# Context transposed once and kept in DRAM, and the first group of the last stage opened in two halves of rows

## What is computed

```python
x = x + L0_xattn(layernorm(x), ctx)        # one head, per sequence
x = x + L0_ffn(layernorm(x))               # 8 experts of 512, best 2 per row, and a shared one
x = x + L1_xattn(layernorm(x), ctx, mask)  # 16 heads of 64: keys and values from ctx
x = x + L1_ffn(layernorm(x))               # relu, 128 -> 512 -> 128
```

## Time and profile before

| | us |
|---|---|
| median of 3 runs | 1432.9 (1428.61 to 1436.73) |
| the profiled execution: its time | 1434.55 |
| the profiled execution: its span | 1432.9 |
| PE busy in it | 1315.9 (92%) |
| DVE, ACT, POOL busy in it | 983.2, 779.6, 523.0 |

### The profile page before, as it was taken

How to read it: one execution, slowest core, us unless ns; L and a number is a source line. 1 busy time by engine, 2 the same in 40 slices (tenths; PEclk the granted TensorE clock), 3 DMA queues, 4 the chain that set the end, 5 groups by cost and what they waited for, 6 DMA issues and landing times.

```text
span 1432.9 us, 41859 instructions
## 1 busy us (share of the span) xinstructions
PE 1315.9 (92%) x16184; PEld 1149.3 (80%) x16185; DVE 983.2 (69%) x2418; ACT 779.6 (54%) x1480; POOL 523.0 (36%) x560
## 2 busy tenths in 40 slices
PE   4999999985999999757899999999999999999977
PEld 3888888874999999745787888788878888888866
DVE  3788888765655555425787778777877777778673
ACT  3455555532555555335565656656665666566642
POOL 2366666653122222273424342434243424331000
PEclk9899999997999999969999999999999999999998
DMA  3111112604222222120110111011101110110000
GB/s 85 40 59 60 60 60 64 183 30 120 78 77 77 76 78 73 59 70 25 28 28 15 29 35 28 14 31 33 30 13 31 32 31 14 31 28 13 2 9 16
DMA packets 90348, 66.85 MB, mean 47 GB/s; under 512 B 24816, under 2 KB 81136, under 8 KB 90192
## 3 DMA queue, kind: packets, MB, share of 16 engines
q1 hardware_dynamic: 78592, 38.51, 9.5%
q0 software_dynamic: 11600, 26.10, 6.1%
HBM read 40.73 MB, written 23.86 MB: 45 GB/s over the span
## 4 chain that ended last, share of the span: by engine, by line
PE 48%; DVE 3%; issue 2%; POOL 2%; ACT 1%; DMA 0%; another core or an unknown queue 0%; DVEq 0%; ACTq 0%; POOLq 0%
PE c_ps_w L83 21%; PE c_ps_w L1414 8%; PE c_ps_s L1380 5%; PE c_ps_w L1403 5%; PE c_ps_w L1431 4%; PE c_ps_w L1389 3%; PE c_ps_w L1333 2%; POOL c_back L1262 1%; DVE c_shifted L1711 1%; DVE c_shifted L1708 1%; DVE c_r_max L1710 1%; POOL k_X L1272 0%; DMA c_back<-sorted_y,k_y_row_of 0%; ACT c_o_t L1563 0%
## 5 line engine op out<-in xcount | busy, mean ns | idle before, releaser
L1283 POOL TENSOR_TENSOR c_rstd<-c_var,c_minus_half 128x1 f32<-128x1 f32 x64 | 35.8, 560 | 484.0 <-DVE c_var L1691 484.0
L91 POOL DMA_INDIRECT sorted_x<-f_XN,f_slot_of x128 | 130.7, 1021 | 81.4 <-PE a_ps_w L749 30.7
L1414 PEld LDWEIGHTS c_ps_w<-c_wo,c_o_t 128*128 128x128 f32 x1024 | 124.7, 196 | 24.1 <-ACT c_o_t L1563 20.9
L1414 PE MATMUL c_ps_w<-c_wo,c_o_t 128*128 128x128 f32 x1024 | 129.5, 281 | 14.4 <-ACT c_o_t L1563 10.9
L1262 POOL DMA_INDIRECT c_back<-sorted_y,k_y_row_of x128 | 125.9, 983 | 39.0 <-issue 34.8
L1535 ACT ACTIVATE c_q_t<-c_ps_w 128x512 f32<-128x512 f32 x128 | 74.5, 602 | 117.7 <-PE c_ps_w L83 116.3
L1055 PE MATMUL d_ps_y<-e_w_all,d_h_t 128*128 x1136 | 138.1, 275 | 0.3 <-ACT d_h_t L1009 0.3
L1055 PEld LDWEIGHTS d_ps_y<-e_w_all,d_h_t 128*128 128x128 f32 x1136 | 132.8, 192 | 0.5 <-issue 0.5
L1708 DVE TENSOR_TENSOR c_shifted<-c_ps_s,c_mask 128x1024 f32<-128x1024 f32 x64 | 78.4, 1224 | 76.6 <-PE c_ps_s L1380 70.9
L940 POOL DMA_DIRECT2D sorted_y<-d_y_rows x71 | 51.9, 731 | 210.8 <-DVE d_y_rows L971 206.5
L1009 ACT ACTIVATE d_h_t<-d_ps_h,d_biases 128x256 f32<-128x256 f32 x284 | 111.4, 475 | 4.4 <-PE d_ps_h L83 4.2
(11 more groups left out here) (238 smaller groups left out, 3545.8 us busy)
## 6 DMA issues: line engine op xcount, KB each, us to landing
d_x_rows<-sorted_x SPq DMA_DIRECT2D x71, 128.0 KB, 2.1
sorted_y<-d_y_rows POOLq DMA_DIRECT2D x71, 128.0 KB, 2.2
k_X<-in_x SPq DMA_DIRECT2D x16, 256.0 KB
a_q_rows<-in_ctx SPq DMA_DIRECT2D x16, 256.0 KB
c_ctx_rows<-in_ctx SPq DMA_DIRECT2D x16, 256.0 KB
out<-k_X SPq DMA_DIRECT2D x16, 256.0 KB, 2.3
sorted_x<-f_XN,f_slot_of POOLq DMA_INDIRECT x128
e_w_all<-in_L_ffn_w SPq DMA_DIRECT2D x1, 2048.0 KB
```

Of the source, the lines that this page charges most:

```text
L91: pool.indirect_dma_start(out=sorted_x, out_offset=bass.IndirectOffsetOnAxis(ap=slot_of[:, choice, t:t + 1], axis=0), in_=XN2[:, t, :], in ...
L1414: last = pe.matmul(w[:, 0:D], o_t[:, j, :], wo[:, j, :], start=(j == 0), stop=(j == J - 1))
```

## The change

1. **Context kept.** Stage a stores each `q_t` (the transposed context) to DRAM as `ctx_cols[g]` with a transfer of SP; ACT's next write of `q_t` waits for it (`ctx_stored`). Stage c loads `ctx_cols[g]` into `ctx_raw` and splits from there: its 16 sets of four context transposes and their PSUM banks are gone. `XN2` becomes a ring of four groups (`xn2`), whose reuse waits for the scatters.
2. **Experts' weights earlier.** SP issues them after the loads that follow groups 5, 8, 11 and 12 of stage a.
3. **Stage d.** Eleven tiles are written out. The four `low` parts are made one after each of tiles 3 to 6; the context of group 0 is loaded and split there (ACT after tile 7, DVE after tile 8). DVE copies the first three tiles' weights ahead of its first `low_x`. ACT runs one `Gelu` on a single column before its first copy.
4. **Opening of stage c.** Group 0's rows are added by DVE tile by tile (`add_first`), and normalised, transposed and projected in two halves of two tiles (`xna`, `xnb`; `qa`, `qb`), with scores(0) between them. Keys, values and queries of group 1 are placed among tiles 0 to 3. Group 1 is gathered into the unused `h_t`.

The core of the diff:

```diff
+            for g in range(G):
+                sp.wait_ge(ct_ready, 3 * g + 3)
+                sp.dma_start(ctx_cols[g], q_t[:]).then_inc(ctx_stored, 16)
...
+                if g >= 1:
+                    act.wait_ge(ctx_stored, 16 * g)
                 act.wait_ge(full, full_at("qt", g))
                 act.copy(q_t[:], bank("qt", g)[:]).then_inc(ct_ready, 1)
...
+def high_context(act, ctx_t, raw):
+    c = batches_of(raw)
+    act.copy(ctx_t.high[:, :, 0:NB, :], c)
+    return act.copy(ctx_t.high[:, :, NB, :], c[:, :, 0, :])
...
+                if 3 <= n < 3 + len(layer1):
+                    low_layer1(n - 3)
+                if n == 8:
+                    dve.wait_ge(ctx_high, 1)
+                    low_context(dve, ctx_t, ctx_raw).then_inc(ctx_low, 1)
...
+            def add_first(k):
+                dve.wait_ge(gathered_0[k], 16 * 2)
+                for choice, w in enumerate((w_first, w_second)):
+                    step(dve.scalar_tensor_tensor(row_of(k), back[:, choice, k, :], w[:, k:k + 1], row_of(k), ALU.mult, ALU.add))
...
-            ctx_transposes(0)
             project_k(0, range(J))
-            for p in range(GT):
+            for p in range(GT - 1):
                 project_v(p, range(2))
+            first_transposes("xna", 0)
+            project_v(GT - 1, range(2))
+            project_first("qa", 0)
+            scores(0)
+            project_k(1, (0, 1))
+            first_transposes("xnb", 1)
+            project_k(1, (2, 3))
+            project_first("qb", 1)
+            scores(1)
+            project_k(1, (4, 5))
+            transpose_probs(0)
+            project_k(1, (6, 7))
+            values(0)
+            project_v(GT, range(2))
             pe.wait_ge(w_loaded, 16 * 4)
-            xn_transposes(0)
-            project_q(0, range(J))
+            out_projection(0)
+            scores(2)
+            transpose_probs(1)
+            project_v(GT + 1, range(2))
+            values(1)
             xn_transposes(1)
-            ctx_transposes(1)
+            project_v(GT + 2, range(2))
+            out_projection(1)
+            project_q(1, (0, 1, 2, 3))
+            scores(3)
...
-                if k == 3 and g + 2 < G:
-                    ctx_transposes(g + 2)
```

More of the change, by code:

```diff
@@ L100, in phase_a @@
     MAX_TILES = NT * P // SLOTS
[L101 removed]
+    BANKS, AHEAD, KEPT = 8, 3, 4
     with ExitStack() as ctx:
@@ new lines, in filled @@
+            yield ("xna", 0)
+            yield from (("v", GT - 1, h) for h in range(2))
+            yield from (("qa", 0, n) for n in range(J // 2))
+            yield from (("k", 1, j) for j in (0, 1))
+            yield ("xnb", 0)
+            yield from (("k", 1, j) for j in (2, 3))
+            yield from (("qb", 0, n) for n in range(J // 2))
+            yield from (("k", 1, j) for j in (4, 5))
+            yield from (("pt", 0, half) for half in range(2))
+            yield from (("k", 1, j) for j in (6, 7))
@@ L1136, in filled @@
+            yield from (("q", 1, j) for j in (4, 5))
+            yield from (("pv", 2, b) for b in range(NB))
+            yield from (("q", 1, j) for j in (6, 7))
+            yield ("o", 2)
+            yield from (("v", GT + 3, h) for h in range(2))
+            yield ("xn", 2)
+            for p in range(GT, NT):
                 yield from filled_in_slot(p)
@@ L1153, in filled_in_slot @@
                 yield from (("k", g + 1, j) for j in (5, 6))
-            if k == 3 and ended:
+            if k == 3:
                 yield ("down", g - 1, 0)
-            if p > 0:
-                yield from (("pt", p - 1, half) for half in range(2))
+            yield from (("pt", p - 1, half) for half in range(2))
             if k == 0 and coming:
@@ L1334, in transposes, with first_transposes @@
                 last.then_inc(full, 1)
-            def ctx_transposes(g):
-                pe.wait_ge(loaded, 16 * (g + 1))
-                transposes(begin("ctx", g), ctx_rows)
+            def first_transposes(name, half):
+                ks = range(half * GT // 2, (half + 1) * GT // 2)
+                pe.wait_ge(x_normed, ks[-1] + 1)
+                w = begin(name, 0)
+                for n, k in enumerate(ks):
+                    last = pe.transpose(w[:, n * P:(n + 1) * P], xn_rows[:, k, :], ident[:])
+                last.then_inc(full, 1)
             def xn_transposes(g):
@@ L1346, in x4_transposes, with project_first @@
                 transposes(begin("x4", g), xn4_rows)
+            def project_first(name, half):
+                emptied(("xna", "xnb")[half], 0)
+                HW = GW // 2
+                for n in range(J // 2):
+                    w = begin(name, 0, n)
+                    for a in range(2):
+                        j = 2 * n + a
+                        last = split_matmul(pe, w[:, a * HW:(a + 1) * HW], wq, xn_t, lambda c: c[:, j * P:(j + 1) * P],
+                                            lambda x: x[:, half * HW:(half + 1) * HW])
+                    last.then_inc(full, 1)
             def project_q(g, js):
@@ L1528, in high_x4, with take_first @@
                 act.copy(xn_t.high[:], bank("x4", g)[:]).then_inc(high_ready, 1)
+            def take_first(name, half):
+                HW = GW // 2
+                for n in range(J // 2):
+                    act.wait_ge(full, full_at(name, 0, n))
+                    act.mul(q_t[0][:, 2 * n:2 * n + 2, half * HW:(half + 1) * HW],
+                            bank(name, 0, n)[:].rearrange("p (a c) -> p a c", a=2), Q_SCALE).then_inc(free_of(name, 0, n), 1)
             def take_q(g, js):
```

457 lines of the change are left out of this document (294 added, 163 removed).

## The result

The changed kernel takes 1423.5 us (median of 4 runs, 1422.5 to 1426.1) against 1433.0 for the kernel before (4 runs). The ratio is 0.9935, with a 95% interval of 0.9917 to 0.9954: 9.4 us or 0.65% faster. Forecast were 1403 (1391 to 1420). The profiled execution took 1424.52 us, its span is 1422.7.

A forecast was written before the change was run, and what follows sets the result against it. The prediction took PE as the bound inside the stages, with PE's waits at the stage borders as the rest. Terms -22.4 - 5.0 - 2.3 = -29.7 us from the median 1432.9 gave 1403 us, range 1391 to 1420.

The forecast's parts named there:

- Opening, -22.4: Opening of stage c: new order laid out on traced times brings scores(4) earlier; -22.4 us, bounds 14 to 31.3.
- The rival of DVE's chain: Opening of stage c: DVE's serial chain becomes the new bound, gaining only 5 to 14 us; 1411 to 1421, chance 0.17.
- Middle, -5.0: Middle of stage c: PE is the bound, so removing four context transposes in 13 groups gives -5.0 us, bounds 0 and 5.7.
- The rival "the idle time only changes place": Stage c: the opening's waits return in groups 1 and 2, whose gathers POOL does later; 1428 to 1436, chance 0.05.
- Stage d, -2.3: Stage d, 376 to 380: low parts spread one per tile hide beside the loop, removing 2.35 us of PE idle; -2.3 us.
- Stage a, 0: Stage a: ACT's wait for the store of `q_t` and the earlier weight loads cost nothing; 0, from -1 to +3 us.
- Sum: Whole kernel: opening, middle and stage d together, -22.4 - 5.0 - 2.3 = -29.7 us.
- the scores of tile 4 came in time: Sign in stage c's opening: scores(4) expected near 673; the prediction is wrong if they come after 685.
- DVE's time did not grow: Sign in stage c: the prediction is wrong if DVE's time in a group grows.
- A group's period near 47.6: Sign in the middle of stage c: a group's period expected near 47.6 us, where it was 48.1.
- the border at 603 to 604: Sign at stage c's border: expected 2.3 us earlier, if stage a and the start of stage d stand.

The follow-up runs named there:

- e7: e4 with the gathers in group 1's slots and the two ahead of its sums also set between the short matmul runs; 1379.7 us, ratio 0.9608.
- e5: Kernel before, with only POOL's gathers in a group's second and third slot waiting until PE has done the slot's values; 1406.6 us, ratio 0.9787.
- e4: Changed kernel, with POOL's gathers in the second and third slot of groups 2 to 12 waiting for the slot's values; 1391.8 us, ratio 0.9687.
- e10: e5, with ACT copying the previous tile's values ahead of its exp in a group's first slot; 1398.5 us, ratio 0.9701.
- e9: e7, with ACT copying the previous tile's values ahead of its exp in a group's first slot; 1366.4 us, ratio 0.9492.
- e12: Changed kernel as it is, run once more; 1428.2 us, ratio 0.9915 to the kernel before.
- e8: Changed kernel, with the gathers of groups 3 to 15 replaced by plain POOL transfers of 128 rows (wrong rows); 1383.3 us, ratio 0.9640.

## Why the prediction was wrong

The direction was right, the size was not: 9.4 us instead of 29.7. By its own steps:

- **Opening, -22.4.** Right in order and size. Measured -21.3, from the end of stage d to tile 4. The order of events was as written: keys to scores(0) 18.4 us (laid out 18.3), the 4.2 us of waiting for group 1's rows (laid out 4). Keys to scores(4) took 71.5 us instead of 67.4; those 4 us are scores(1), held up by gathers, and without most of that (e7) tiles 0 to 4 take 4.1 us less. The rival of DVE's chain did not come true. The low part of the context, now made from SBUF, takes DVE 1.1 us a group as before, so the contention of two SBUF inputs that the Trainium skill warns of ("SBUF — State Buffer", "Who interferes with whom") did not arise there.
- **Middle, -5.0.** This step failed: "PE is the bound there". Measured +9.2 in groups 2 to 12. Its bounds were 0 and 5.7, no loss among them, because the 70 us that DVE waits for PE's scores were read as PE at work. A part of them was PE held up by POOL's gathers, a cost that the sum does not have: 2.2 us of each 48.1 (48.08 to 45.85 in e5) before the change and 2.9 after it. A second piece was hidden in the same sentence: in the slot from which the transposes went PE waits for a copy on ACT, so that they gave nothing (e4 against e5) until the order on ACT was changed. Then they gave 0.51 a group (e10 to e9), where 0.44 was laid out. That the held-up time itself grew, by 0.7 a group, is in the timelines, not in an experiment of its own: the values in the third slot are now cut in two,

```profile
1005.04 1.34 PE L1528 MATMUL c_ps_w<-c_p_t,c_v_s 64*64 64x64 f32 x50
1006.76 0.49 PE L1528 MATMUL c_ps_w<-c_p_t,c_v_s 64*64 64x64 f32 x14 [0.37 <-issue]
```

  because the gather beside them comes later in the slot, the one before it having taken 2.00 us:

```profile
1003.23 2.00 POOL L1345 DMA_INDIRECT c_back<-sorted_y,k_y_row_of  x1 [0.17 <-issue]
1005.53 0.96 POOL L1345 DMA_INDIRECT c_back<-sorted_y,k_y_row_of  x1 [0.30 <-issue]
```

- **The rival "the idle time only changes place".** It named the right place (groups 3 and 4 gathered later, POOL's order tight) and was set aside for the wrong reason, that POOL is busy 17.8 of 48.1 us. POOL had time enough. What counted was beside which matmuls its gathers ran: group 1 lost 8.9 us (57.1 instead of 48.2), and with the gathers moved it takes 47.0 in the changed kernel (e7) and 46.0 in the kernel before (e5).
- **Stage d, -2.3.** Measured -1.8 (254.60 to 252.80). The hole at 376 to 380 is closed:

```profile
376.00:380.00 4.00, 4.00 (x37) 4.00 (x37) 3.37 (x9) 3.23 (x9) 0.71 (x1) 1.00 0.36 111
```

- **Stage a, 0.** ACT waits for no transfer of `q_t` there. The border lay 3.4 us earlier in the first profile, by scatter for the most part (e12).
- **Sum.** With the gathers out of the way and ACT's order mended in both kernels, the difference is 32.1 us (e10 1398.5 to e9 1366.4, on the same chip; the runs of each spread over 5 to 6 us); without the order on ACT 26.9 (e5 to e7). So the forecast of 29.7 was about what the edits are worth in such a kernel. That it lies between the two is in part luck, since the middle's share comes only with an order on ACT that the prediction did not look at. What it missed is what the edits did to a stall that was in the kernel all along.

The stall could have been seen before the change, but hardly in the rows on record. Scores(0) in the earlier trace rows, 57 matmuls in 1.86 us where scores(4) take 1.16 for 64, were slow for another reason, the clock. The window of that row:

```profile
655.61:657.47 1.86, 1.86 (x58) 1.67 (x57) 1.43 (x3) 0.86 (x2) 1.45 (x2) 0.50 0.19 55
```

Only that 7 of the 64 are missing from the row points at the gathers: they follow behind two short gaps marked issue. The page of the kernel before names the stall plainly, in the line of its scores:

```profile
L1380 PE MATMUL c_ps_s<-c_k_t,c_q_t 64*64 64x64 f32 x4096 | 86.5, 226 | 12.3 <-issue 12.3
```

All idle time ahead of the scores is issue there. Group 13 (tiles 52 to 56) does nearly the same work as the groups before it but gathers nothing, and takes 45.85 us instead of 48.1 in the same profile. The prediction did not ask about either. Nor do its signs catch it: the scores of tile 4 came in time and DVE's time did not grow. A group's period near 47.6 failed, and so did the border at 603 to 604 (keys at 600.67), but that one by the start of stage d.

## What to carry to other kernels

A busy share near 97% does not show that an engine is at full speed. Compare equal groups of instructions with each other, look at the granted clock of each first, and then for gaps marked issue inside them. Where POOL makes gathers while PE runs many short matmuls, put the gathers beside long ones by a wait on PE's own progress: it cost two lines here and gave 2% (e5). When work taken from the fullest engine gives nothing, look at the queue order of the engine that it waits for in that slot.

## What the hardware did that was not expected

While POOL's indirect transfers (128 rows of 512 bytes, 1.27 us from one to the next) are under way, PE is slow in runs of 64x64 matmuls: 64 of them took 3.05 us beside two gathers and 1.09 without, and the last 28 matmuls of the values of tile 6 took 4.8 us (719.4 to 724.2) beside six in a row. Beside four in a row a pass of DVE began 2.1 us after its input was there. Matmuls of 512 columns beside gathers show no such gaps, and plain transfers of as many rows from POOL's queue do none of it (e8). The Trainium skill ("SBUF — State Buffer", "Who interferes with whom") says that PE and ACT never wait on anyone. As a statement on ports no run here contradicts it; as a rule for reading a timeline it does not hold, since PE lost 2.2 us of 48.1 in each group to POOL's gathers. What of an indirect transfer reaches PE's instructions (the reading of the addresses, the making of the single transfers, or the way by which instructions come) was not separated and stays open. A packet of instructions on its way is not it in the case above: from 1000.7 to 1003.8 us of the kernel before the instruction queue moves none.
